# Small products of an in-kernel eigen-solver on all 128 rows of TensorE, its counting passes cut into quarters, and new places for both in the instruction order

## Chip, cores and metric

One Trainium2 chip, one core. The time is device microseconds of one launch (us), the median of the runs; one further execution was profiled.

## What is computed

The input is x of 128 graphs x 64 nodes x 128 features, and one 64 x 64 adjacency matrix for all graphs. Four residual layers follow one another, each fed by relu(layer norm(x)):

```python
x = x + L0(h, adj)   # graph convolution, two batch norms
x = x + L1(h, adj)   # two graph convolutions, then LSTMs over windows of 1, 2, 3 and 4 nodes
x = x + L2(h, adj)   # uses U of this:
    deg = sum(A, 0) + sum(A, 1) - diagonal(A)
    L_norm = dinv[:, None] * (diag(deg) - A) * dinv[None, :]
    _, U = eigh(L_norm)
    out = U @ (relu((U.T @ h) @ W1 + b1) @ W2 + b2)
x = x + L3(h, adj)   # three convolutions, 128 -> 256 -> 512 -> 128
```

The change touches only the eigendecomposition of one symmetric 64 x 64 matrix and the places of its instructions among those of L0 and L1.

## The kernel before, in words

Tokens are worked on in 4 iterations of 2048, each of 4 chunks of 512. L0 and L1 run first; L2 and L3 are one last stage ("D stage"), which needs U, as `BDU`, for its first products. All data is f32, and each matmul stands in the trace as two passes, each with its own weight load (LDWEIGHTS, engine PEld).

The eigen-solver runs beside L0 and L1, mostly on VectorE (DVE):

- 62 Householder reflections reduce the matrix `S` to a tridiagonal one. `S` has 128 rows: rows 0 to 63 are the matrix, rows 64 to 127 collect the transformation. In L0 (`reflection_beside_l0`, 28 reflections) each asks TensorE for `row_product` (L476) and `av_product` (L487); in L1 (`reflection`, 34 reflections) for one pair, `old_row` (L483) and `av_product`. Their stationary operand is a column broadcast to 128 columns, `S[0:NODES, k:k+1]`, `ident[0:NODES, ...]` or `vcol[0:NODES]`: 64 rows of the array. DVE signals `vcol` and the last column of `S` (L1289, L1290; in L0 L1208, L1212) and goes on at L1303 (L1225 in L0) when the product is there.
- `tail`: two rounds of counting. Each runs a recurrence over `Z` (128 x 65 x 32), then three passes over all of `Z`: a comparison (L1407), a comparison of neighbours (L1410) and a sum (L1414); a small product (`counts`, `sc`) follows, already with 128 rows. Then the "twist" (128 dependent tiny steps), a product of `both_ways`, the eigenvectors `V` (L1539), and six pairs or single products of 64 rows that polish U.

TensorE, DVE and ScalarE (ACT) execute in program order, so the order is the schedule. In L1, LSTM gate products are the bulk of TensorE's work: per round two sets q, each with 3 or 4 gates, of 512, 336 or 256 columns. Between gates stand "tasks" of the next or the previous chunk: `turn` and `turn_h` (transposes, 4 per chunk), `agg`, `g0`, `g1`, `agg2`. All tasks use one PSUM bank, `task_bank`; a task waits until the last one's result was taken. For `turn` and `turn_h` DVE takes it, by the addition `X<-X,PS` (L1878); for `agg2` by `T<-PS,RB` (L1817), which ACT then turns into the LSTM's input (L890).

Where the solver's instructions stand is laid out by clocks kept while the program is written. TensorE's clock (`spend`) adds the columns of each gate; when it passes `due`, the next small product is sent, `SMALL` is added, and `PACE...` gives the distance to the next. DVE's clock adds `DVE_STEP` per solver step and `busy(us)` for long ones; at each step `beside_l1` puts in at most one of L1's DVE instructions (an addition, a `BN_STATS`, a `BN_AGGR`, ...) whose time has come.

Of the kernel before, what the change touches and what calls it, by code (L numbers as in the profile page):

```python
# [21 lines left out]
ALU = mybir.AluOpType  # L22
ACT = mybir.ActivationFunctionType
AX = mybir.AxisListType.X

P = 128
GRAPHS, NODES, D = 128, 64, 128
# [14 lines left out]
M = 32  # L42
# [177 lines left out]

PACE = 3.6
PACE_AV = 6.7
PACE_GRID = [47.0, 43.0]
PACE_TWIST = 40.0
PACE_SCAN = 14.0
PACE_LAST = 8.0

SMALL = 0.5

DVE_STEP = {"reflect": 0.24, "grid": 0.16, "twist": 0.27, "tail": 0.21}  # L230

# [3 lines left out]

BEGINS = 0.5

PASS = 2.1

LN_STEP = 0.5  # L240

# [14 lines left out]
def build(nc, x_in, cst_in, w_in, adj_in, out):  # L256
    ctx = ExitStack()
    with ctx:
        def sb(name, shape):
            return ctx.enter_context(nc.sbuf_tensor(name, shape, F32))  # L260

        def sem(name):
            return ctx.enter_context(nc.semaphore(name))
# [9 lines left out]
        def C(name):  # L273
            return cst[:, coff[name][0]:coff[name][1]]
# [36 lines left out]
        S = sb("S", [P, NODES + 1])  # L311

        NI = sb("NI", [P, NODES + 2])
        vcol = sb("vcol", [P, 1])
# [9 lines left out]
        Z = sb("Z", [P, NODES + 1, M])  # L324
# [34 lines left out]
        hh_S, hh_x, hh_row, hh_v, hh_av = sem("hh_S"), sem("hh_x"), sem("hh_row"), sem("hh_v"), sem("hh_av")  # L359
# [53 lines left out]
        def eb(n):  # L413

            return PS[:, 6, n * P:(n + 1) * P]
# [35 lines left out]
        def _(pe):  # L451
            begin(pe, pe_done, pe_set)

            def mm(o, l, r, start=True, stop=True):
                return nc.tensor.matmul(o, l, r, start=start, stop=stop)  # L455

            ident = C("ident")
# [19 lines left out]
            def row_product(k):  # L477

                pe.wait_ge(hh_x, k + 1)
                mm(eb(0)[:, 0:NODES + 1 - k], S[0:NODES, k:k + 1].broadcast_to((NODES, P)),  # L480
                   NI[0:NODES, k + 1:NODES + 2]).then_inc(hh_row, 1)

            def old_row(o, k):  # L483

                n = NODES - 1 - k
                return mm(o[:, 0:n], ident[0:NODES, k:k + 1].broadcast_to((NODES, P)), S[0:NODES, k + 1:NODES])

            def av_product(k):

                pe.wait_ge(hh_v, k + 1 + max(0, k + 1 - REFLECTED))  # L490
                if REFLECTED <= k < REFLECTIONS - 1:
                    old_row(eb(3), k + 1)
                mm(eb(2)[:, 0:NODES - k], vcol[0:NODES, 0:1].broadcast_to((NODES, P)), S[0:NODES, k + 1:NODES + 1])\
                    .then_inc(hh_av, 1)

            def eigen_products(lo):


                for k in range(lo, REFLECTIONS):
                    yield PACE_AV  # L500
                    av_product(k)
# [6 lines left out]
                for n in range(ROUNDS):  # L508
                    yield PACE_GRID[n]
                    pe.wait_ge(grid_cnt, n + 1)  # L510
# [5 lines left out]

                yield PACE_TWIST
                pe.wait_ge(prep_dve, PREP["ways"])
# [63 lines left out]
            for r in range(REFLECTED):  # L582
                m = r - L0_FIRST
# [22 lines left out]

            pe.wait_ge(hh_S, REFLECTED + 1)
            old_row(eb(0)[:, (REFLECTED % 2) * NODES:], REFLECTED).then_inc(hh_row, 1)

            small = eigen_products(REFLECTED)  # L610
# [3 lines left out]
            def send():  # L614
                pace = next(small, None)
                sent.append(clock[0])
                clock[0] += SMALL
                due[0] = None if pace is None else max(due[0], clock[0] - 1.0) + pace
# [424 lines left out]
        def _(dve):  # L1043
            begin(dve, dve_done)
            v = nc.vector
# [9 lines left out]
            def busy(us):  # L1055

                dclock[0] += us

            def beside_l1(kind):

                busy(DVE_STEP[kind])
                if before_next() and l1_next[0] + lag[0] <= dclock[0]:
                    l1_next[0] = next(l1[0], None)
# [27 lines left out]
            ident, blocks = C("ident"), C("blocks")  # L1091
# [229 lines left out]
            def tail():  # L1321
# [24 lines left out]
                cn = counts[:, 0:M]  # L1346
                g = [0]

                def gop(ins):
                    g[0] += 1  # L1350
                    ins.then_inc(grid_ops, 1)

                def gsync(back=0):
                    beside_l1("grid")
                    dve.wait_ge(grid_ops, g[0] - back)

                gop(v.memset(counts[:, M:M + 1], 1.0))
                for r in range(ROUNDS):
# [45 lines left out]
                    gsync(1)  # L1404
                    gop(v.tensor_tensor(tb, Z[:, NODES, :], tb, ALU.mult))
                    gsync()
                    gop(v.tensor_scalar(Z[:, 0:NODES, :], Z[:, 0:NODES, :], 0.0, None, ALU.is_lt))  # L1407
                    gsync()
                    busy(3 * PASS)
                    gop(v.tensor_tensor(Z[:, 0:NODES - 1, :], Z[:, 0:NODES - 1, :], Z[:, 1:NODES, :], ALU.not_equal))  # L1410
                    gsync()
                    gop(v.scalar_tensor_tensor(Z[:, NODES - 1, :], xg[:, :], -1.0, tb, ALU.mult, ALU.is_gt))
                    gsync()
                    gop(v.tensor_reduce(cn, Z[:, 0:NODES, :].rearrange("p i m -> p m i"), AX, ALU.add))  # L1414
                    gsync()
                    if r == 0:

                        lanes = C("lanes").unsqueeze(1).broadcast_to(pair)
# [29 lines left out]
                ratio, inv, a, gam, hot, zt, zb, mul, t2 = (Fq[:, n, :] for n in range(9))  # L1448
# [436 lines left out]
            for k in range(REFLECTED, REFLECTIONS):  # L1885
                reflection(k)
            tail()
            assert taken[0] == len(sent)
            for _ in l1[0]:
# [109 lines left out]
```

## Time and profile before

| | |
|---|---|
| time, median of 3 runs | 953.56 us (953.52 to 959.08) |
| the profiled execution | 955.17 us, span 953.4 us |
| PE busy | 849.2 us (89%) |
| PEld busy | 558.3 us (59%) |
| DVE busy | 564.5 us (59%) |
| ACT busy | 517.3 us (54%) |
| POOL busy | 315.7 us (33%) |
| chain that ended last | PE 57%, DVE 14%, ACT 4%, POOL 2% |

The span is divided roughly so: L0 to 157 us, the passage to L1 to 178 us, L1 to 633 us, the D stage to the end. The last reflection's products are at 404 us, the counting rounds end at 461 and 506 us, the last product of the solver is at 589 us. Busy shares are averages; what a part of the change is worth is read at its place, from gaps between starts and from the waits. PEclk is TensorE's granted clock, 1.0 for 2.4 GHz and 0.5 for 1.2 GHz.

### The profile page before, as it was taken

Reading aid. Unit: us, or ns where it says so; the run is one execution under the profiler, and the core shown is the slowest. Engines: PE = TensorE matmul, PEld = TensorE weight load, DVE = VectorE, ACT = ScalarE, POOL = GpSimd, SP = SyncE. Lnnn points to the kernel's source line nnn. Section 1 sums busy time; section 2 is a strip of 40 time slices with the busy share of each in tenths; the row PEclk is TensorE's granted clock in tenths of the full one; section 3 lists DMA queues with packets and bytes.
Section 4 is the critical chain, followed back from the end, with each engine's and each line's share of the span. In section 5 each row is a group of like instructions: output and inputs, shape, how many; then the busy total and the mean of one; then the engine's idle time right before and its main releaser. Section 6 shows DMA issues by size and latency. Waiting matters only on the chain.

```text
span 953.4 us, 12338 instructions
## 1 busy us (share of the span) xinstructions
PE 849.2 (89%) x3723; PEld 558.3 (59%) x3723; DVE 564.5 (59%) x3050; ACT 517.3 (54%) x958; POOL 315.7 (33%) x373
## 2 busy tenths in 40 slices
PE   2777597798999889996899799988999999999998
PEld 1444344644687446863467545766568658858847
DVE  5899878799678977799886858436015005204101
ACT  1566585575656555664565455675364463454521
POOL 1333201375556544565564566004003002202000
PEclk9999898899999989998999899999999999999999
DMA  8000000000000000000000000000001000000101
GB/s 348 0 1 1 1 0 1 1 0 1 1 1 0 1 2 0 1 1 1 0 1 1 1 1 1 0 1 1 1 1 45 1 1 14 32 0 2 45 1 45
DMA packets 3395, 13.27 MB, mean 14 GB/s; under 512 B 512, under 2 KB 512, under 8 KB 2688
## 3 DMA queue, kind: packets, MB, share of 16 engines
q1 hardware_dynamic: 3328, 12.48, 3.3%
q8 instruction: 30, 0.49, 0.2%
q14 instruction: 37, 0.30, 0.1%
HBM read 8.28 MB, written 4.19 MB: 13 GB/s over the span
## 4 chain that ended last, share of the span: by engine, by line
PE 57%; DVE 14%; ACT 4%; POOL 2%; issue 1%; ACTq 0%; DVEq 0%
PE PS L455 56%; POOL BIG L1002 1%; ACT BIG L911 1%; DVE X L1878 1%; ACT T L877 1%; DVE Fq L1475 1%; DVE seg L1476 1%; ACT T L823 1%; PE PS L641 1%; DVE stats L1651 1%; DVE PS L1369 1%; DVE PS L1371 1%; DVE Z L1376 1%; DVE Z L1373 0%; ACT BIG L934 0%
## 5 line engine op out<-in xcount | busy, mean ns | idle before, releaser
L455 PE MATMUL PS<-BIG,wts 128*128 128x512 f32 (+2 forms) x952 | 341.3, 501 | 9.4 <-ACT BIG L911 7.0
L1002 POOL TENSOR_TENSOR BIG<-BIG 128x256 f32<-128x256 f32 (+2 forms) x220 | 211.0, 967 | 162.5 <-ACT BIG L911 96.2
L455 PEld LDWEIGHTS PS<-BIG,wts 128*128 128x128 f32 x952 | 177.4, 193 | 132.1 <-issue 95.9
L911 ACT ACTIVATE BIG<-PS,lbias 128x256 f32<-128x256 f32 (+2 forms) x312 | 162.6, 559 | 113.7 <-PE PS L455 111.6
L455 PE MATMUL PS<-H,wts 128*128 128x256 f32 (+2 forms) x312 | 115.0, 494 | 9.1 <-POOL H L1002 4.7
L815 ACT ACTIVATE BIG<-PS 128x1024 f32<-128x1024 f32 x64 | 65.5, 1023 | 88.5 <-PE PS L455 88.5
L815 ACT ACTIVATE T<-PS 128x512 f32<-128x512 f32 x96 | 55.7, 594 | 91.6 <-PE PS L455 91.3
L455 PE MATMUL PS<-T,wts 128*128 128x512 f32 x192 | 101.1, 648 | 1.7 <-ACT T L815 1.5
L1878 DVE TENSOR_TENSOR X<-X,PS 128x512 f32<-128x512 f32 x64 | 43.2, 679 | 99.3 <-PE PS L455 87.1
L979 POOL TENSOR_SCALAR rstd<-mv 128x4 f32<-128x4 f32 x48 | 11.0, 228 | 266.0 <-DVE mv L1679 266.0
L1925 DVE TENSOR_TENSOR T<-PS,wts 128x512 f32<-128x512 f32 x16 | 11.1, 691 | 142.9 <-PE PS L455 142.9
L823 ACT ACTIVATE T<-X,shift,rstd 128x128 f32<-128x128 f32 x192 | 78.4, 482 | 25.8 <-DVE shift L1688 25.8
L455 PEld LDWEIGHTS PS<-H,wts 128*128 128x128 f32 x312 | 57.6, 197 | 42.2 <-issue 19.8
L934 ACT ACTIVATE BIG<-BIG 128x512 f32<-128x512 f32 (+2 forms) x88 | 44.8, 510 | 49.1 <-POOL BIG L1002 48.3
L455 PE MATMUL PS<-wts,T 128*128 128x128 f32 (+1 forms) x384 | 60.6, 311 | 0.2
L455 PEld LDWEIGHTS PS<-wts,T 128*128 128x128 f32 x384 | 55.3, 191 | 6.8 <-issue 1.9
L455 PEld LDWEIGHTS PS<-wts,BIG 128*128 128x128 f32 x512 | 57.8, 192 | 1.9 <-issue 1.9
L455 PE MATMUL PS<-wts,BIG 128*128 128x128 f32 x512 | 57.8, 275 | 0.0
L455 PEld LDWEIGHTS PS<-T,wts 128*128 128x128 f32 x192 | 34.4, 199 | 30.6 <-issue 22.8
L981 POOL TENSOR_TENSOR rstd<-rstd,cst 128x4 f32<-128x4 f32 x48 | 49.8, 1038 | 4.0
L1672 DVE BATCH_NORM_STATS2 stats<-X 128x6 f32<-128x128 f32 x208 | 46.6, 278 | 0.7
L971 POOL TENSOR_TENSOR sc<-sc,cst 128x1 f32<-128x1 f32 x28 | 15.3, 548 | 93.8 <-DVE sc L1197 93.8
(318 smaller groups left out, 1194.9 us busy)
## 6 DMA issues: line engine op xcount, KB each, us to landing
X<-x_in SPq DMA_DIRECT2D x4, 1024.0 KB, 16.8
out<-X SPq DMA_DIRECT2D x16, 256.0 KB, 2.0
wts<-w_in SPq DMA_DIRECT2D x1, 3542.0 KB, 13.7
cst<-cst_in SPq DMA_DIRECT2D x1, 419.0 KB, 3.5
AA<-adj_in SPq DMA_DIRECT2D x2, 16.0 KB, 2.1
```

The lines of the kernel that those rows point to most:

```text
L455: return nc.tensor.matmul(o, l, r, start=start, stop=stop)
L815: nc.scalar.activation(dst, src, fn, **kw).then_inc(act_done[k], 1)
L823: j = nc.scalar.activation(T0[:, k, t * P:(t + 1) * P], X[:, a:a + P], ACT.Relu, bias=shift[:, k, t:t + 1], scale=rstd[:, k, t:t + 1])
L911: nc.scalar.activation(LB[:, q, {"i": I_, "g": G_, "f": F_, "o": O_}[g], 0:n], PS[:, 3 * q + rank[q] % 3, 0:n], ACT.Tanh if g == "g" else ...
L934: nc.scalar.activation(LB[:, q, I_, 0:n], LB[:, q, CELL, 0:n], ACT.Tanh).then_inc(act_set[q], 1)
L971: return nc.gpsimd.tensor_tensor(o, ap, mh[:, 0:1] if e is None else e, ALU.pow)
L979: nc.gpsimd.tensor_scalar(rstd[:, k, :], mv[:, k, :, 1], EPS, None, ALU.add).then_inc(pool_done[k], 1)
L981: nc.gpsimd.tensor_tensor(rstd[:, k, :], rstd[:, k, :], mh[:, 0:TPC], ALU.pow).then_inc(pool_done[k], 1)
L1002: nc.gpsimd.tensor_tensor(out, a, b, op).then_inc(pool_set[q], 1)
L1672: j = v.bn_stats(stats[:, k, t, :], X[:, a:a + P])
L1878: v.tensor_tensor(x, x, src, ALU.add).then_inc(dve_done[k], 1)
L1925: v.tensor_tensor(by_tile(T1[:, k, 0:CH]), by_tile(bank(k)), W("l2b2row").unsqueeze(1).broadcast_to(four), ALU.add).then_inc(dve_done[k], 1)
```

## The change

The three products of the reflections take all 128 rows of `S`, `NI`, `ident` and `vcol`; rows 64 to 127 of one operand are zero there (`NI` and `ident[:, k]` for k < 64, `vcol`), so the sums are the same. The three counting passes are cut into four instructions each, over quarters of the nodes (512 elements) or, for the sum, of the 32 lanes, each followed by a step in which one instruction of L1 may stand. `PASS`, `PACE_GRID`, `PACE_TWIST` and `SMALL` change the clocks by which places are laid out.

```diff
--- before.py
+++ after.py
@@ -220,12 +220,12 @@
 
 PACE = 3.6
 PACE_AV = 6.7
-PACE_GRID = [47.0, 43.0]
-PACE_TWIST = 40.0
+PACE_GRID = [52.0, 37.0]
+PACE_TWIST = 38.0
 PACE_SCAN = 14.0
 PACE_LAST = 8.0
 
-SMALL = 0.5
+SMALL = 0.45
 
 DVE_STEP = {"reflect": 0.24, "grid": 0.16, "twist": 0.27, "tail": 0.21}
 
@@ -235,7 +235,8 @@
 
 BEGINS = 0.5
 
-PASS = 2.1
+PASS = [0.25, 0.6, 0.75]
+QUARTER = NODES // 4
 
 LN_STEP = 0.5
 
@@ -477,21 +478,19 @@
             def row_product(k):
 
                 pe.wait_ge(hh_x, k + 1)
-                mm(eb(0)[:, 0:NODES + 1 - k], S[0:NODES, k:k + 1].broadcast_to((NODES, P)),
-                   NI[0:NODES, k + 1:NODES + 2]).then_inc(hh_row, 1)
+                mm(eb(0)[:, 0:NODES + 1 - k], S[:, k:k + 1].broadcast_to((P, P)), NI[:, k + 1:NODES + 2]).then_inc(hh_row, 1)
 
             def old_row(o, k):
 
                 n = NODES - 1 - k
-                return mm(o[:, 0:n], ident[0:NODES, k:k + 1].broadcast_to((NODES, P)), S[0:NODES, k + 1:NODES])
+                return mm(o[:, 0:n], ident[:, k:k + 1].broadcast_to((P, P)), S[:, k + 1:NODES])
 
             def av_product(k):
 
                 pe.wait_ge(hh_v, k + 1 + max(0, k + 1 - REFLECTED))
                 if REFLECTED <= k < REFLECTIONS - 1:
                     old_row(eb(3), k + 1)
-                mm(eb(2)[:, 0:NODES - k], vcol[0:NODES, 0:1].broadcast_to((NODES, P)), S[0:NODES, k + 1:NODES + 1])\
-                    .then_inc(hh_av, 1)
+                mm(eb(2)[:, 0:NODES - k], vcol[:, 0:1].broadcast_to((P, P)), S[:, k + 1:NODES + 1]).then_inc(hh_av, 1)
 
             def eigen_products(lo):
 
@@ -1404,15 +1403,22 @@
                     gsync(1)
                     gop(v.tensor_tensor(tb, Z[:, NODES, :], tb, ALU.mult))
                     gsync()
-                    gop(v.tensor_scalar(Z[:, 0:NODES, :], Z[:, 0:NODES, :], 0.0, None, ALU.is_lt))
-                    gsync()
-                    busy(3 * PASS)
-                    gop(v.tensor_tensor(Z[:, 0:NODES - 1, :], Z[:, 0:NODES - 1, :], Z[:, 1:NODES, :], ALU.not_equal))
-                    gsync()
+                    for a in range(0, NODES, QUARTER):
+                        busy(PASS[0])
+                        gop(v.tensor_scalar(Z[:, a:a + QUARTER, :], Z[:, a:a + QUARTER, :], 0.0, None, ALU.is_lt))
+                        gsync()
+                    for a in range(0, NODES, QUARTER):
+                        b = min(a + QUARTER, NODES - 1)
+                        busy(PASS[1])
+                        gop(v.tensor_tensor(Z[:, a:b, :], Z[:, a:b, :], Z[:, a + 1:b + 1, :], ALU.not_equal))
+                        gsync()
                     gop(v.scalar_tensor_tensor(Z[:, NODES - 1, :], xg[:, :], -1.0, tb, ALU.mult, ALU.is_gt))
                     gsync()
-                    gop(v.tensor_reduce(cn, Z[:, 0:NODES, :].rearrange("p i m -> p m i"), AX, ALU.add))
-                    gsync()
+                    for a in range(0, M, M // 4):
+                        busy(PASS[2])
+                        gop(v.tensor_reduce(cn[:, a:a + M // 4],
+                                            Z[:, 0:NODES, a:a + M // 4].rearrange("p i m -> p m i"), AX, ALU.add))
+                        gsync()
                     if r == 0:
 
                         lanes = C("lanes").unsqueeze(1).broadcast_to(pair)
```

The count of instructions on ACT, POOL and SP and their order do not change; TensorE runs the same matmuls; DVE has 18 instructions more.

DVE, round 0, from the end of the recurrence to the first `turn_h` addition (X<-X,PS), before:

```order
L1405 TENSOR_TENSOR PS<-Z,PS 128x32
L1651 BN_STATS stats<-X 128x6
L1407 TENSOR_SCALAR Z<-Z 128x2048
L1410 TENSOR_TENSOR Z<-Z 128x2016
L1651 BN_STATS stats<-X 128x6
L1412 SCALAR_TENSOR_TENSOR Z<-xg,PS 128x32
L1651 BN_STATS stats<-X 128x6
L1414 TENSOR_REDUCE counts<-Z 128x32
L1651 BN_STATS stats<-X 128x6
L1420 TENSOR_SCALAR tmp<-cst,counts 128x128
L1421 TENSOR_SCALAR sc<-sc 128x1
L1878 TENSOR_TENSOR X<-X,PS 128x512
```

The same place with the change, where the first such addition is the seventh row:

```order
L1404 TENSOR_TENSOR PS<-Z,PS 128x32
L1408 TENSOR_SCALAR Z<-Z 128x512
L1657 BN_STATS stats<-X 128x6
L1408 TENSOR_SCALAR Z<-Z 128x512
L1657 BN_STATS stats<-X 128x6
L1408 TENSOR_SCALAR Z<-Z 128x512
L1884 TENSOR_TENSOR X<-X,PS 128x512
L1408 TENSOR_SCALAR Z<-Z 128x512
L1657 BN_STATS stats<-X 128x6
L1413 TENSOR_TENSOR Z<-Z 128x512
L1657 BN_STATS stats<-X 128x6
L1413 TENSOR_TENSOR Z<-Z 128x512
```

And further on, to the second addition:

```order
L1413 TENSOR_TENSOR Z<-Z 128x480
L1657 BN_STATS stats<-X 128x6
L1415 SCALAR_TENSOR_TENSOR Z<-xg,PS 128x32
L1657 BN_STATS stats<-X 128x6
L1419 TENSOR_REDUCE counts<-Z 128x8 x2
L1663 BN_AGGR mv<-stats 128x2
L1419 TENSOR_REDUCE counts<-Z 128x8
L1884 TENSOR_TENSOR X<-X,PS 128x512
L1419 TENSOR_REDUCE counts<-Z 128x8
```

Before, the first addition stood behind all passes; now it stands inside the first pass, and the second one (right behind the first, but for statistics, before) behind three quarters of the sum.

PE, from the last LSTM iteration's rounds of 512 columns to the product of `V` (Fq), before:

```order
L455 MATMUL PS<-H,wts 128x512 x11
L455 MATMUL PS<-both_ways,cst 128x128
L455 MATMUL PS<-H,wts 128x512 x4
L641 MATMUL PS<-cst,BIG 128x128 x4
L455 MATMUL PS<-H,wts 128x512 x3
L641 MATMUL PS<-cst,BIG 128x128 x4
L455 MATMUL PS<-H,wts 128x512 x3
L455 MATMUL PS<-BIG,wts 128x512
L522 MATMUL PS<-cst,Fq 64x64
L525 MATMUL PS<-cst,S 64x64
```

and with the change:

```order
L456 MATMUL PS<-H,wts 128x512 x8
L456 MATMUL PS<-both_ways,cst 128x128
L456 MATMUL PS<-H,wts 128x512 x7
L640 MATMUL PS<-cst,BIG 128x128 x4
L456 MATMUL PS<-H,wts 128x512 x3
L640 MATMUL PS<-cst,BIG 128x128 x4
L456 MATMUL PS<-H,wts 128x512
L521 MATMUL PS<-cst,Fq 64x64
L524 MATMUL PS<-cst,S 64x64
L456 MATMUL PS<-H,wts 128x512 x2
```

The product of `both_ways` stands three gate products earlier against the gates, that of `Fq` too; the `turn_h` transposes (cst,BIG) stand where they stood against the gates.

DVE at the same part of the program, where L1539, now L1545, writes V; the first addition in the rows below is that of `turn_h` chunk 1. Before:

```order
L1537 TENSOR_SCALAR sc<-sc 128x1
L1538 TENSOR_SCALAR sc<-sc 128x1
L1878 TENSOR_TENSOR X<-X,PS 128x512
L1539 TENSOR_SCALAR Fq<-Fq,sc 128x64
L1553 COPY EV<-PS 64x64
L1554 COPY EV<-PS 64x128
L1878 TENSOR_TENSOR X<-X,PS 128x512
```

and with the change:

```order
L1543 TENSOR_SCALAR sc<-sc 128x1
L1544 TENSOR_SCALAR sc<-sc 128x1
L1545 TENSOR_SCALAR Fq<-Fq,sc 128x64
L1884 TENSOR_TENSOR X<-X,PS 128x512 x2
L1559 COPY EV<-PS 64x64
L1560 COPY EV<-PS 64x128
L1563 COPY EV<-PS 64x64
```

The addition of `turn_h` chunk 0 stood 16 solver instructions before V, outside the upper piece; it has moved behind V and stands right ahead of that of chunk 1.

Elsewhere: in round 0 the product of `counts` stands 5 gate products of 512 columns and one of 336 later, that of `sc` (round 1) one gate product of 256 columns and one task of 4 x 128 columns earlier; the first product of the tail (EV,cst) one gate product of 256 columns later. The four `T<-PS,RB` additions in the twist stand 9, 12, 12 and 8 solver instructions later, counted without the 18 new ones. In the reflections single additions move by up to four solver instructions earlier.

## Rows read from the trace of the kernel before

**Rows 1.** Windows by stage, core 0: busy us (x instructions) of each engine, PEclk, DMA share, GB/s.
```profile
108.00:157.00 49.00, 41.30 (x105) 18.02 (x104) 37.72 (x188) 34.54 (x50) 5.83 (x11) 0.90 0.00 1
178.00:404.00 226.00, 213.23 (x905) 138.45 (x903) 182.58 (x1263) 134.48 (x264) 121.84 (x124) 0.98 0.00 1
...
437.00:475.00 38.00, 27.75 (x78) 14.42 (x77) 31.18 (x130) 16.19 (x31) 19.28 (x16) 0.82 0.00 1
475.00:546.00 71.00, 63.50 (x277) 45.52 (x276) 57.08 (x248) 40.24 (x86) 38.25 (x46) 0.95 0.00 1
...
633.00:953.40 320.40, 312.39 (x1648) 223.27 (x1648) 71.23 (x306) 147.29 (x242) 35.25 (x56) 0.99 0.04 14
```

**Rows 2.** Waits, 178 to 404 us: waiter <- waited for: us in total, times, longest.
```profile
DVE sc L1303 <- PE PS L455: 37.2, 22, 4.3
...
PE PS L455 <- DVE S L1290: 7.0, 5, 2.2
```

**Rows 3.** Timeline around the small products at 304 us: start, length, instruction, [idle before].
```profile
302.32 2.31 PE L455 MATMUL PS<-H,wts 128*128 128x512 f32 x5
...
302.70 0.27 DVE L1290 TENSOR_SCALAR S<-S,sc 128x1 f32<-128x1 f32 x1
...
304.56 0.39 PE L455 MATMUL PS<-S,cst 64*128 64x15 f32 x2
...
305.10 0.30 PEld L455 LDWEIGHTS PS<-H,wts 128*128 128x128 f32 x2
...
305.64 0.19 PEld L455 LDWEIGHTS PS<-H,wts 128*128 128x128 f32 x1 [0.24 <-issue]
```

**Rows 4.** Timeline of PEld at 461 us, around two small products of 128 rows.
```profile
461.61 0.19 PEld L455 LDWEIGHTS PS<-counts,tmp 128*128 128x128 f32 x1 [0.24 <-issue]
...
461.94 0.30 PEld L455 LDWEIGHTS PS<-BIG,wts 128*128 128x128 f32 x2
462.48 0.19 PEld L455 LDWEIGHTS PS<-BIG,wts 128*128 128x128 f32 x1 [0.24 <-issue]
```

**Rows 5.** Timeline of PE, 45.5 to 48.6 us.
```profile
45.92 0.43 PE L455 MATMUL PS<-S,vcol 64*128 64x59 f32 x2 [0.62 <-DVE S L1212]
...
48.23 0.43 PE L455 MATMUL PS<-NI,S 64*128 64x59 f32 x2 [0.80 <-DVE NI L1191]
```

**Rows 6.** Timeline of PE and DVE, 127.2 to 132.5 us.
```profile
128.90 0.41 PE L455 MATMUL PS<-NI,S 64*128 64x44 f32 x2
...
131.20 0.08 DVE L1212 DVE_READ_ACCUMULATOR2_ANT S<- 128x1 f32 x1
...
132.01 0.41 PE L455 MATMUL PS<-S,vcol 64*128 64x43 f32 x2
```

**Rows 7.** Timeline of DVE, 437.5 to 450 us: the counting passes of round 0.
```profile
438.20 1.28 DVE L1407 TENSOR_SCALAR Z<-Z 128x2048 f32<-128x2048 f32 x1
439.51 3.20 DVE L1410 TENSOR_TENSOR Z<-Z 128x2016 f32<-128x2016 f32 x1
...
443.14 3.59 DVE L1414 TENSOR_REDUCE counts<-Z 128x32 f32<-128x2048 f32 x1
...
447.15 0.68 DVE L1878 TENSOR_TENSOR X<-X,PS 128x512 f32<-128x512 f32 x1
```

**Rows 8.** Timeline of PE, 436.5 to 476 us.
```profile
447.88 1.12 PE L641 MATMUL PS<-cst,H 128*128 128x128 f32 x4 [7.82 <-DVE X L1878]
448.80 6.94 PE L455 MATMUL PS<-BIG,wts 128*128 128x512 f32 x10
```

**Rows 9.** Timeline of DVE, 500 to 546 us: first and last of four additions L1817.
```profile
515.04 0.68 DVE L1817 TENSOR_TENSOR T<-PS,RB 128x512 f32<-128x512 f32 x1
...
534.68 0.68 DVE L1817 TENSOR_TENSOR T<-PS,RB 128x512 f32<-128x512 f32 x1
```

**Rows 10.** Timeline of PE and DVE, 553 to 567.5 us.
```profile
553.79 0.22 DVE L1503 TENSOR_TENSOR Fq<-PS,Fq 128x64 f32<-128x64 f32 x1 [7.78 <-PE PS L455]
...
566.59 0.24 PE L522 MATMUL PS<-cst,Fq 64*64 64x64 f32 x1 [0.28 <-DVE Fq L1539]
```

## Prediction

> **What bounds the kernel now.** I read the windows by stage first [rows 1]: from 178 to 404 us PE is busy 213.2 of 226 us at a granted clock of 0.98, while DVE stands at 81% and ACT and POOL at 60% or less. The D stage from 633 us on holds no instruction that the change touches; its 320.4 us stay. So the question is what TensorE does between 108 and 633 us, and where it stands still.
>
> Second, the waits of the reflections inside L1 [rows 2]. DVE waits 37.2 us in 22 stretches for a small product, PE waits for DVE's `S` in only 5 of 34 reflections (7.0 us). The solver is thus paced by TensorE's order in most reflections: a small product is due before TensorE reaches it, and its whole cost lies on the path.
>
> Third, that cost, from starts in the timeline [rows 3]. The passes of 512 columns follow at 0.43 us. Five begin at 302.32, so the last one ends its columns at 302.32 + 5 x 0.43 = 304.46. The next pass of 512 columns has its weight load at 305.10 and the one after it at 305.64; that one starts with the end of the pass before, so the pass's columns began at 305.64 - 0.43 = 305.21. The pair costs 305.21 - 304.46 = 0.75 us, although DVE was ready from 302.97 on, 1.6 us ahead. The first small pass starts about 0.1 us after the columns before it ended (304.56 against 304.46), with no weights loaded ahead of it.
>
> Two small products that already use 128 rows stand at 461 us [rows 4]: the last gate pass ends at 461.61, the next one begins at 462.48 - 0.43 = 462.05. Their cost is 0.44 to 0.45 us, four passes at 0.11: no gap before, none behind, weights loaded ahead.
>
> **Small products in L1 (34 pairs).** By these two rows a pair falls from 0.75 to 0.45, by 0.30. Where PE waits for DVE anyway (5 by the list; I take 6) the next reflection starts at most 0.1 earlier. 28 x 0.30 + 6 x 0.1 = 9.0. Of this I take back 1.2, four pairs' worth, for places where TensorE soon waits for POOL's or ACT's part of a round, whose chain began before the pair: 7.8. Bounds: nothing, if rows are not what makes the difference, and 34 x 0.30 = 10.2.
>
> The row shows a stop before and a late load behind a product of 64 rows between products of 128. The Trainium skill, TensorEngine Tiling (Array Packing), Key Properties, says that changing the tiling mode drains TensorE, and names 64 rows as another mode than 128. By that rule each pair pays twice; the trace agrees, 0.75 against 0.45.
>
> **Small products in L0.** In its first part (19 reflections) PE stands idle 0.62 and 0.80 us ahead of each small product, waiting for DVE [rows 5]. The array is empty then, nothing can be loaded ahead, and the chain is DVE's: 0, at most 19 x 0.1 = 1.9 from the free exit. In the second part [rows 6] `row_product` starts at 128.90, DVE signals at 131.28, and `av_product` starts only at 132.01: three gate-like halves (six passes, 2.56) lie between. Here PE is waited for, by 0.73. The product's result comes 0.2 earlier (0.1 drain, 0.1 load), and the exit of `row_product` takes 0.1 less: 0.3 per reflection. Eight of them: 2.5 (bounds 0 and 8 x 0.6 = 4.8). DVE's slack of 0.73 covers it.
>
> **Counting passes, round 0.** TensorE stopped 7.82 us before 447.88 [rows 8], because the addition that empties `task_bank` stood behind 1.28 + 3.20 + 3.59 us of passes [rows 7]. After it ten passes took 6.94 us instead of some 4.4: half clock, 2.5 lost. Together 10.5. The granted clock in 437 to 475 us is 0.82 [rows 1].
>
> With the change the first addition stands behind three quarters of the comparison. Three more recurrence steps and one more BN_STATS stand ahead: the passes begin about 0.6 late, at 438.8. Pieces of the comparison take 0.4 to 0.5, a BN_STATS between two about 0.2, so the addition starts at 438.8 + 3 x 0.4 + 2 x 0.2 = 440.4 instead of 447.15, 6.75 earlier: the stop shrinks to 1.1. But then the second addition is late. TensorE needs it one transposition and five gate products later: 441.2 + 0.4 + 5 x 0.86 = 445.9. Before it DVE has the last comparison piece with statistics (0.6 + 0.6 for the addition itself), four neighbour pieces with a BN_STATS each (3.20 / 4 plus a fixed part and 0.2, about 1.0 each: 4.0), 0.5 of small ones, and three quarters of the sum (3.59 / 4 + 0.1, 1.0 each) with a BN_AGGR: 440.4 + 1.2 + 4.0 + 0.5 + 3.1 = 449.2, done by 449.9. TensorE waits 3.8 to 4, and I charge the half clock again, 2.5. So 1.1 + 3.8 + 2.5 = 7.4 instead of 10.5: **3.1 saved**. Bounds: 10.5 if the pieces are shorter than I think and the second wait fades, -2 if both stops bring the half clock. Moving the product of `counts` into TensorE's wait at the next round start hides its 0.45: 0.4 more. The wait of DVE before its round 1 is not on the path, and the product of `sc` comes 0.43 + 0.86 = 1.3 earlier in TensorE's order; in round 1 nothing of L1 waits for the passes, and their some 1 us of added fixed cost falls into DVE's idle time ahead of `sc`.
>
> **Twist.** The four additions `T<-PS,RB` pace TensorE: ACT, in order, waits for each, and gates wait behind ACT. They run from 515.04 to 534.68 [rows 9], 82 solver steps and three additions of 0.6 apart, so 0.22 per step. They move 9, 12, 12 and 8 steps later, but the whole chain begins 1.3 earlier. The last one decides: 8 x 0.22 - 1.3 = +0.4 us. Bounds -1.3 and +1.8.
>
> **Tail.** `both_ways` is sent three gate products (2.6) earlier. DVE had waited 7.78 us for it [rows 10], so it is ready. V came 13.3 us after the product (553.3 to 566.6); without the two additions now behind it, 12.1. V is then there 2.6 + 1.2 earlier and 0.4 later, at 563.2; the addition of chunk 0 follows and ends at 563.9. TensorE wants it at about 562.3: 1.6 of waiting where 0.25 was, less the 0.3 that it waited for V before: **1.0 lost**. Bounds 0 and 3.5 (with a half clock).
>
> **Sum.** -7.8 - 2.5 - 3.1 - 0.4 + 0.4 + 1.0 = -12.4. The profiled span of 953.4 becomes 941.0. The profiled execution took 955.17, 1.6 above the median of 953.56; since two of three runs lie at 953.5, I set the change against the median: 941.2.
>
> **Rivals.**
> 1. *Rows do not matter.* The gap at 304 us could belong to the broadcast column or to the pair's place in the queue. For it: the pair at 461 us has other operands and DVE far ahead. Against it: both load 128 columns. Then only the last four terms stay, -2.1: 951.5. The Trainium skill, TensorE: Matmul & The Clock Gate, section LDWEIGHTS, gives a load's time by its columns alone and says that the count of rows doesn't matter; by this page the edit would change nothing. The passes of a pair do follow at the same 0.11 us with 64 and with 128 rows, which agrees, but the rule is silent on the entry and the exit, and there the rows differ.
> 2. *The counting stop goes entirely.* If pieces and statistics take a third less, the second addition is in time and the clock stays up: 6.3 more, 934.9. Against it: the measured 3.59 for the sum leaves little room.
> 3. *Late additions make it slower.* The mechanism: each addition delays its own round, and the delays add up instead of moving with DVE's chain. The four in the twist would cost (9 + 12 + 12 + 8) x 0.22 = 9.0, the one behind V 16 x 0.22 = 3.5, and two stops at half clock 2.5 each: 17.5, and the counting passes give nothing back. Against the 10.3 of the reflections: +7.2, 960.8, with some 4 to both sides. It decides only if TensorE stands waiting at every one of the four; against it, additions that stand closer together cannot each be late.
>
> **Chances.** My forecast 0.70, rival 1 0.14, rival 2 0.11, rival 3 0.05. The forecast's own spread, from the bounds, is 936 to 948; the range goes to 934 below and to 950 above, which leaves most of rival 1 and all of rival 3 outside. One per cent, 9.5 us, is about what can be told from no change here: under 944.0 lie rival 2 and four fifths of my own case, 0.67; over 963.1 a third of rival 3, 0.02; the rest, 0.31, lies within.
>
> **What would show it.** Around a pair, the next pass of 512 columns should begin 0.45 us after the last one ended, with its weight load 0.11 behind the small one's. In the second part of L0 `av_product` should start 2.9 after `row_product`, not 3.1 [rows 6]. The last pair should stand at 394 instead of 404 us; if it is at 404, the first two terms are wrong. Between 437 and 475 us there should be two stops of PE for X L1878, of 1 and 4 us, the second followed by half clock; one stop or none is rival 2. The four T additions should keep their spacing, and `turn_h` chunk 1 should wait 1.6 for the addition behind V.

## The result: 948.97 us, 5.0 less, where 12.4 were forecast

| | before | after |
|---|---|---|
| median of the runs (9 each) | 954.00 us | 948.97 us (944.69 to 950.66) |
| ratio after / before, 95% interval | | 0.994 (0.9921 to 0.9959) |
| the profiled execution, its span | 955.17, 953.4 | 947.86, 946.1 |
| PE busy | 849.2 us (89%) | 837.5 us (89%) |
| DVE busy | 564.5 us | 571.5 us |
| chain that ended last | PE 57%, DVE 14% | PE 55%, DVE 15% |

The time lies in the range, and the gain is less than half of the one forecast. The interval of the ratio leaves out 1, so the kernel is faster, though by less than the 1% that the prediction took as its bound. Measured again beside other kernels the ratio was 0.9931 (0.9906 to 0.9956).

**Windows by stage** of the changed kernel, columns as in [rows 1]:

```profile
178.00:404.00 226.00, 212.39 (x935) 144.28 (x935) 186.78 (x1279) 137.45 (x268) 126.80 (x130) 0.97 0.00 1
...
437.00:475.00 38.00, 32.06 (x110) 18.93 (x109) 32.26 (x157) 21.09 (x44) 17.16 (x16) 0.91 0.00 0
475.00:546.00 71.00, 60.58 (x254) 41.37 (x253) 62.33 (x249) 39.79 (x82) 40.23 (x47) 1.00 0.00 1
```

The last number but two is the granted clock. That of the counting stretch is up from 0.82 to 0.91, that of the twist from 0.95 to 1.00; in the reflections it is down, 0.97 against 0.98, though more matmuls are done.

**A pair of small products**, PE and PEld at 301 us, where [rows 3] show one of 64 rows:

```profile
299.45 1.88 PE L456 MATMUL PS<-H,wts 128*128 128x512 f32 x4
301.16 0.29 PE L456 MATMUL PS<-S,cst 128*128 128x15 f32 x2
```

The weight loads of the same moment:

```profile
300.74 0.19 PEld L456 LDWEIGHTS PS<-S,cst 128*128 128x128 f32 x1 [0.24 <-issue]
...
301.50 0.30 PEld L456 LDWEIGHTS PS<-H,wts 128*128 128x128 f32 x2
302.04 0.19 PEld L456 LDWEIGHTS PS<-H,wts 128*128 128x128 f32 x1 [0.24 <-issue]
```

Four passes of 0.43 from 299.45 end at 301.17: the small product follows with no gap, its weights loaded from 300.74 on. The gates' columns are back at 302.04 - 0.43 = 301.61. The pair costs 0.44 instead of 0.75.

**The counting passes of round 0**, DVE's timeline, for [rows 7]:

```profile
431.06 0.43 DVE L1408 TENSOR_SCALAR Z<-Z 128x512 f32<-128x512 f32 x1
431.40 0.29 DVE L1657 BATCH_NORM_STATS2 stats<-X 128x6 f32<-128x128 f32 x1
431.60 1.32 DVE L1408 TENSOR_SCALAR Z<-Z 128x512 f32<-128x512 f32 x1
432.84 0.28 DVE L1657 BATCH_NORM_STATS2 stats<-X 128x6 f32<-128x128 f32 x1
433.04 1.28 DVE L1408 TENSOR_SCALAR Z<-Z 128x512 f32<-128x512 f32 x1
434.24 0.67 DVE L1884 TENSOR_TENSOR X<-X,PS 128x512 f32<-128x512 f32 x1
434.84 1.50 DVE L1408 TENSOR_SCALAR Z<-Z 128x512 f32<-128x512 f32 x1
```

POOL's timeline of the same stretch:

```profile
431.36 2.68 POOL L1001 TENSOR_TENSOR BIG<-BIG 128x512 f32<-128x512 f32 x2 [0.74 <-ACT BIG L933]
434.78 1.28 POOL L1001 TENSOR_TENSOR BIG<-BIG 128x512 f32<-128x512 f32 x1 [0.74 <-ACT BIG L933]
```

A quarter of the comparison takes 0.43 us alone. The three that begin while POOL is at work end 0.28 us after POOL's instruction (for the last two, POOL ends at 434.04 and 436.06, the pieces at 434.32 and 436.34) and take 1.28 to 1.50. Together 4.5 us, where the whole comparison took 1.28. TensorE's stops that follow, for [rows 8]:

```profile
434.97 0.71 PE L640 MATMUL PS<-cst,H 128*128 128x128 f32 x4 [2.68 <-DVE X L1884]
443.71 0.92 PE L640 MATMUL PS<-cst,H 128*128 128x128 f32 x4 [3.74 <-DVE X L1884]
```

**The tail**, PE from 537 to 575 us, for [rows 10]:

```profile
537.93 0.38 PE L456 MATMUL PS<-both_ways,cst 128*128 128x128 f32 x2
...
544.22 2.84 PE L456 MATMUL PS<-H,wts 128*128 128x512 f32 x6 [2.48 <-POOL H L1001]
...
551.34 0.71 PE L640 MATMUL PS<-cst,BIG 128*128 128x128 f32 x4 [1.03 <-DVE X L1884]
...
552.85 0.24 PE L521 MATMUL PS<-cst,Fq 64*64 64x64 f32 x1
...
573.41 2.28 PE L456 MATMUL PS<-H,wts 128*128 128x336 f32 x4 [2.22 <-POOL H L1001]
```

`turn_h` waits 1.0 for the addition behind V, but two round starts wait 2.5 and 2.2 us for POOL as well (1.45 and 1.60 before), and behind the second the clock falls: windows give 0.84 for 575 to 582 us.

Starts of the same instructions in the two traces give the account by stretch; a product that stands earlier in TensorE's order is set back by the gate columns it was moved past (1.3 us at `sc`, 2.56 at `both_ways`):

| stretch | forecast | profile | second profile |
|---|---|---|---|
| L0, to the last `row_product` (156.8, 154.4) | -2.5 | -2.3 | -3.9 |
| reflections in L1 (to 407.1, 398.9) | -7.8 | -5.8 | -7.8 |
| counting, with the product of `counts` (to 506.3, 494.4) | -3.5 | -2.4 | -2.4 |
| twist (to 553.3, 537.9) | +0.4 | -2.2 | -2.2 |
| tail, to the first `BDU` product (633.8, 625.0) | +1.0 | +3.9 | +3.9 |
| D stage | 0 | +1.5 | +1.5 |
| sum | -12.4 | -7.3 | -10.9 |

The second profile is of the same kernel (run after_again, 944.28 us); its runs lay at 944.0 to 944.3 (four) and at 948.3 to 952.7 (five). The two profiles part in L0 (granted clock 0.70 in one, 0.80 in the other, from 108 to 125 us) and above all between 215 and 250 us, at one pair of small products; see the late pairs below. The profiled execution of before was 1.2 over its median and that of after 1.1 under its own, which is why 7.3 becomes 5.0.

### The profile page after: what moved, and what is told of

It reads as the page before. It is cut to its first block, busy times and chain, and to the rows that moved or that the text cites. A ratio compares the mean times of both kernels' runs of the same rounds, so it can differ in the third digit from the quotient of the medians.

```text
span 946.1 us, 12357 instructions
## 1 busy us (share of the span) xinstructions
PE 837.5 (89%) x3723; PEld 559.4 (59%) x3723; DVE 571.5 (60%) x3068; ACT 516.1 (55%) x958; POOL 312.6 (33%) x373
## 4 chain that ended last, share of the span: by engine, by line
PE 55%; DVE 15%; ACT 5%; POOL 2%; issue 1%; ACTq 0%; DVEq 0%
PE PS L456 54%; POOL BIG L1001 2%; ACT BIG L910 1%; ACT T L876 1%; DVE X L1884 1%; DVE Fq L1481 1%; DVE seg L1482 1%; ACT T L822 1%; DVE stats L1657 1%; PE PS L640 1%; DVE PS L1368 1%; DVE PS L1370 1%; DVE Z L1375 1%; DVE Z L1372 0%; ACT T L814 0%
## 5 line engine op out<-in xcount | busy, mean ns | idle before, releaser
L1001 POOL TENSOR_TENSOR BIG<-BIG 128x256 f32<-128x256 f32 (+2 forms) x220 | 207.9, 953 | 159.8 <-ACT BIG L910 94.2
L456 PE MATMUL PS<-T,wts 128*128 128x512 f32 x192 | 104.3, 667 | 1.5 <-ACT T L814 1.0
```

The source lines that it names most:

```text
L1001: nc.gpsimd.tensor_tensor(out, a, b, op).then_inc(pool_set[q], 1)
```

## Experiments

All times below are medians, compared by their ratio to the kernel before on the same chip (955 us there). First each part of the change alone, then with one part undone.

**Rows alone.**

```diff
+                mm(eb(0)[:, 0:NODES + 1 - k], S[:, k:k + 1].broadcast_to((P, P)), NI[:, k + 1:NODES + 2]).then_inc(hh_row, 1)
...
+                mm(eb(2)[:, 0:NODES - k], vcol[:, 0:1].broadcast_to((P, P)), S[:, k + 1:NODES + 1]).then_inc(hh_av, 1)
```

> The kernel before with nothing changed but the products of the reflections, on 128 rows. Theory A (the forecast's terms hold and what is missing was lost among the places after the reflections): the last pair at 404 us comes some 8.4 us earlier, as in the changed kernel, and nearly all of it is kept: 944 to 947 us. Theory B (every gain in front of a wait is partly given back at the next stop of TensorE, at half clock too): the last pair is 8 us earlier, but the time falls by 5 or less, 949 or more. Theory C (rows do nothing, the gain is the passes'): 953 to 954.

Measured 945.2 us, ratio 0.9902 (0.9879 to 0.9925): -9.4, faster than the changed kernel. The forecast for its two terms was -10.3; by the median, theory A. Its profile is of the slowest of its six runs (951.46 us) and shows a gain of 3.7 only: the last pair is 7.4 us earlier, and 3.8 of that go between 421 and 436 us, with TensorE at half clock (granted 0.80 in 415 to 432 us). Four transpositions take 0.96 to 1.12 us there instead of 0.60 to 0.66:

```profile
424.57 1.12 PE L634 MATMUL PS<-cst,T 128*128 128x128 f32 x4 [0.62 <-DVE X L1876]
...
428.89 0.96 PE L634 MATMUL PS<-cst,T 128*128 128x128 f32 x4
```

So theory B's mechanism exists too, in some executions. The order of TensorE's and DVE's instructions is the same here as before, so the two traces can be set side by side pair by pair: at 24 of the 34 pairs in L1 the gate products around the pair stand 0.28 to 0.31 us closer. The other ten lie beside a wait or a change of the clock.

**Rows undone** (the same lines the other way, in the changed kernel).

> The changed kernel with its reflection products on 64 rows again; passes in pieces and new places stay. Theory A (passes save about 2, places lose about as much or more): 954 to 957 us. Theory B (gains shrink, places cost little): 951 to 953. If passes and places give the 3 that were forecast for them less 1 for the tail: 951.5.

Measured 955.1, ratio 1.0001 (0.9987 to 1.0015), theory A by the time: pieces and places together give nothing.

**Pieces alone** (`PASS` and the three loops of the diff in the kernel before).

> The kernel before with its counting passes in four pieces each and the clock's costs for them, the four numbers of the places as before. Both theories: one stop of TensorE of 7.8 us at 440 becomes two of 2.9 and 3.9, the granted clock in 437 to 475 us rises from 0.82 to about 0.91, gain 2.3 at that place. Theory A: 951 to 952 us. Theory B: what is gained is lost at the round start behind it, 953 to 954.

Measured 953.25, ratio 0.998 (0.9969 to 0.9992): -1.9, between the two theories. Its trace has stops of 2.67 and 2.69 us.

**Places alone.**

```diff
-PACE_GRID = [47.0, 43.0]
-PACE_TWIST = 40.0
+PACE_GRID = [52.0, 37.0]
+PACE_TWIST = 38.0
...
-SMALL = 0.5
+SMALL = 0.45
```

> The kernel before with only the four numbers of the places changed (52, 37, 38 and 0.45), 64 rows and whole passes. Theory A (the places cost what is missing): 956 to 959 us, with longer stops of TensorE at the start of the round that follows the product of both_ways and for chunk 1 of turn_h. Theory B (the places are nearly free): 953 to 955.

Measured 953.3, ratio 0.9978 (0.9962 to 0.9994): -2.1; theory B by its time. Of A's two stops the first is there (2.4 us for POOL behind `both_ways`, 1.45 before, with half clock behind it), the one for chunk 1 of `turn_h` is not. The places gain at another spot and lose behind `both_ways`. PE in this run, where the kernel before waits 7.82 [rows 8]:

```profile
444.74 0.74 PE L641 MATMUL PS<-cst,H 128*128 128x128 f32 x4 [4.17 <-DVE X L1878]
```

With whole passes the addition now stands between the second and the third. Pieces and places cure the same stop, so their gains don't add. The starts of the same gate products in the traces, against the kernel before, show it for the stretch from 420 to 506 us (the -2.4 of the account above is for a longer one, from 407 us on):

| | change of the stretch, us |
|---|---|
| pieces alone, old places | -3.3 |
| places alone, whole passes | -4.3 |
| rows and places, whole passes (below) | -4.3 |
| pieces and places, with or without the rows | -1.7 |

**The changed kernel again**, as the measure for the next three.

> The changed kernel once more, beside the next three on one chip. If the 5.0 us gained were the draw of a few runs, its ratio leaves 0.992 to 0.996; if not, it is there again. It is the measure for the three kernels beside it.

Measured 948.3, ratio 0.9931: the gain is there again.

**Whole passes in the changed kernel** (the passes' lines of before, rows and places kept).

> The changed kernel with its counting passes whole again; 128 rows and the new places stay. Theory A (the new places alone already put the first addition between the second and the third pass, as in the run of the places alone: one stop of 4.3 us and 1.7 at half clock instead of 2.9 + 3.9 and 1.3; the pieces then cost more than they give): 1 to 2.5 us faster than the changed kernel. Rival (the pieces are worth the 3.1 of the forecast): 3 slower than the changed kernel.

Measured 944.4, ratio 0.9889 (0.9875 to 0.9903): by the median 4 us faster than with the pieces. Its DVE:

```profile
427.38 1.23 DVE L1405 TENSOR_SCALAR Z<-Z 128x2048 f32<-128x2048 f32 x1
...
428.73 3.12 DVE L1408 TENSOR_TENSOR Z<-Z 128x2016 f32<-128x2016 f32 x1
...
432.06 0.68 DVE L1876 TENSOR_TENSOR X<-X,PS 128x512 f32<-128x512 f32 x1
```

The product of `sc` comes 2.7 us earlier than in the second profile of the changed kernel. Behind `both_ways` a stop of 2.7 us for chunk 1 of `turn_h` (1.03 there) and what follows take all of it back: both spans are 942.5 us. The four runs lie at 944.0 to 944.5, as the lower four of the changed kernel do, so the traces give the whole passes nothing in the end. The 4 us of the median stand because five of nine runs of the changed kernel lie at 948.3 to 952.7, and none of four here.

**Only the comparison whole.**

```diff
+                    gop(v.tensor_scalar(Z[:, 0:NODES, :], Z[:, 0:NODES, :], 0.0, None, ALU.is_lt))
+                    for a in range(4):
+                        busy(PASS[0])
+                        beside_l1("grid")
```

> The changed kernel with the comparison as one instruction again, the L1 instructions that stood between its pieces behind it in the same sequence; the other two passes stay in pieces. Theory A (a piece of the comparison that starts while POOL works takes until POOL is done, 1.3 to 1.5 us instead of 0.43; the four took 4.5 us in round 0, the whole 1.28): the first addition comes some 1.9 us earlier, the second some 3, the two stops of TensorE of 2.9 and 3.9 fall to 1.0 and some 2.5: 2.5 to 3.5 us faster than the changed kernel. Rival (the time of those passes is covered by other waits): within 1 us of the changed kernel.

Measured 950.7, ratio 0.9952 (0.9934 to 0.9969): neither theory, 2 us slower. The first stop fell to 1.0 us as expected, the second grew to 4.1, where 2.5 were expected. DVE's timeline:

```profile
432.19 0.67 DVE L1414 TENSOR_TENSOR Z<-Z 128x512 f32<-128x512 f32 x1
...
432.98 1.55 DVE L1414 TENSOR_TENSOR Z<-Z 128x512 f32<-128x512 f32 x1
...
435.45 1.51 DVE L1414 TENSOR_TENSOR Z<-Z 128x480 f32<-128x480 f32 x1
```

Now pieces of the neighbours' comparison wait for POOL: the collisions moved on. Even so the stretch to 506 us is 0.3 us shorter than in the changed kernel; the loss comes behind `both_ways`, where `turn_h` waits 2.68 us for the addition instead of 1.03. Three instructions of V's chain on DVE take 1.11, 1.29 and 1.33 us there, where the changed kernel has 0.25, 0.29 and 1.20.

**The comparison's pieces in another form.**

```diff
-                        gop(v.tensor_scalar(Z[:, a:a + QUARTER, :], Z[:, a:a + QUARTER, :], 0.0, None, ALU.is_lt))
+                        gop(v.tensor_scalar(Z[:, a:a + QUARTER, :], Z[:, a:a + QUARTER, :], 0.0, None, ALU.is_lt, ALU.add,
+                                            accum_out=cn[:, 0:1]))
```

> The changed kernel with its comparison pieces in the form that also writes out a sum of what it compared (into a column that is overwritten later); all else the same. Theory A (the plain form of the piece can't run while POOL works, the form with a sum can): each of the eight pieces takes 0.55 to 0.7 us, whatever POOL does, where three took 1.28 to 1.50 in round 0 and two 1.00 in round 1. Rival (a piece is slow for its own size, or POOL slows any instruction of DVE): pieces beside POOL's work take 1.2 us or more again. Time: within 2 us of the changed kernel, 946 to 949.

Measured 948.1, ratio 0.992 (0.9892 to 0.9949), as expected. DVE's timeline:

```profile
428.70 0.67 DVE L1408 TENSOR_SCALAR_CACHE_REDUCE Z<-Z 128x512 f32<-128x512 f32 x1
...
429.50 0.67 DVE L1408 TENSOR_SCALAR_CACHE_REDUCE Z<-Z 128x512 f32<-128x512 f32 x1
...
431.51 1.75 DVE L1414 TENSOR_TENSOR Z<-Z 128x512 f32<-128x512 f32 x1
```

POOL's:

```profile
428.19 2.50 POOL L1001 TENSOR_TENSOR BIG<-BIG 128x512 f32<-128x512 f32 x2 [0.74 <-ACT BIG L933]
431.44 1.27 POOL L1001 TENSOR_TENSOR BIG<-BIG 128x512 f32<-128x512 f32 x1 [0.74 <-ACT BIG L933]
```

All eight pieces take 0.67 to 0.69 us, seven of them with POOL at work beside them: theory A, the plain form and POOL exclude each other. The first piece of the neighbours' comparison, which reads two operands in SBUF, still waits (1.75). The Trainium skill, SBUF — State Buffer, Who interferes with whom, has this rule: VectorE and GpSimd share one port pair as an exclusive lock; `tensor_scalar` may take it, its form with an accumulator and reductions don't, two SBUF inputs contend with a GpSimd instruction that reads SBUF. The traces agree on each: 1.28 to 1.50, 0.67, 1.5 to 1.75, and 0.99 to 1.08 for each piece of the sum.

**Rows and pieces, old places** (the four numbers as before).

> The kernel before with rows and pieces, the four numbers of the places as before: with the rows alone (ratio 0.990), the passes alone (0.998) and the changed kernel (0.993 to 0.994) beside it. Theory A (the places behind both_ways are what costs): 0.986 to 0.989 of before, 941 to 944 us. Rival (rows and pieces are in each other's way): 0.992 or more.

Measured 948.2, ratio 0.9921 (0.9902 to 0.994): the rival's time. Against rows alone (0.9902) the pieces cost 1.8 by the medians, but the intervals overlap: not settled. From 436 to 506 us the pieces give 0.4 in its trace beside that of rows alone, with stops of 2.68 and 4.31 us, where pieces alone give 3.3 with stops of 2.67 and 2.69.

**The product of `both_ways` back at its place**: `PACE_TWIST = 41.4` for 38.0.

> The changed kernel with PACE_TWIST 41.4 instead of 38: the product of both_ways and what follows stand where they stood before. Theory A (the places behind both_ways cost 4: stops of 2.6, 1.2 and 2.4 us at 541, 550 and 571 us instead of 1.6, 0.3 and 1.8, and a stretch of half clock at 574): 3 to 4 us faster than the changed kernel, the stops as before. Rival (the tail's product only moves the waiting from V to the addition, as forecast, 1.0): 0 to 1 faster.

Measured 941.45, ratio 0.9863 (0.9848 to 0.9879): 6.5 faster than the changed kernel by the medians, more than theory A gave. PE:

```profile
541.21 2.84 PE L456 MATMUL PS<-H,wts 128*128 128x512 f32 x6 [2.49 <-POOL H L1001]
...
566.86 0.33 PE L456 MATMUL PS<-EV,cst 64*64 64x64 f32 x2 [0.57 <-DVE EV L1578]
568.82 3.38 PE L456 MATMUL PS<-H,wts 128*128 128x336 f32 x11 [0.87 <-POOL H L1001]
```

The wait at 541 stays, so that one is not this place's. The waits of 1.0 for the addition and of 2.2 for POOL are gone or halved, and the clock is 1.00 in 575 to 582 us. From `both_ways` to the first `BDU` product it loses 0.7 us where the changed kernel loses 3.9. That is 3.2 us, as theory A had it. The spans differ by 6.3, but 3.0 of these are there before `both_ways`, where the two programs are the same instruction by instruction: they are a difference between executions, and the edit is worth some 3.2 of the 6.5.

**Only the products behind it back**: `PACE_SCAN = 17.4` for 14.0.

> The changed kernel with PACE_SCAN 17.4 instead of 14: the product of both_ways stays early, the product of Fq and all that follow stand where they stood before. Theory A (it is the addition for chunk 1 of turn_h that stands behind DVE's whole chain of V, because that chain is sent early): the stop of 1.2 us at 550 and what follows it stay, 947 to 949 us. Rival (it is the polish products in the gates' order behind it): as fast as with PACE_TWIST 41.4, 941 to 943.

Measured 946.5, ratio 0.9901 (0.9881 to 0.992): between the two theories. By starts the stop at 550 is 1.2 us as in the changed kernel, that at 571 is 1.8 instead of 2.4, and the clock stays at 1.00 behind it. From `both_ways` to the first `BDU` product this trace loses 1.6 us, between 3.9 and 0.7: by it 2.3 of the cost are the products behind, 0.9 the place of `both_ways` itself.

**Whole passes and the old place together** (both edits above).

> The changed kernel with whole counting passes and with PACE_TWIST 41.4, both of the edits that were faster when made alone (944.4 and 941.5 against 948.3). If the whole passes keep the 2.7 us that they are ahead at the product of sc: 938.5 to 939.5. If they are lost again at the next wait, as they were behind both_ways in the run of the whole passes: 941 to 942.

Measured 941.0, ratio 0.9841 (0.982 to 0.9861). Against 0.9863 that is 2 us, with intervals that overlap: not settled.

**The late pairs later.** The two profiles of the changed kernel differ most at one stop. DVE, POOL and PE before the pair at 229 us in the first profile, each in its own timeline:

```profile
223.68 1.28 DVE L1638 SCALAR_TENSOR_TENSOR lnv<-lnv 128x16 f32<-128x16 f32 x1
```
```profile
223.67 3.83 POOL L1001 TENSOR_TENSOR BIG<-BIG 128x512 f32<-128x512 f32 x3 [1.47 <-ACT BIG L910]
```
```profile
229.00 0.62 PE L456 MATMUL PS<-S,cst 128*128 128x26 f32 x2 [3.00 <-DVE S L1289]
```

and the same three in the second profile:

```profile
223.01 0.17 DVE L1638 SCALAR_TENSOR_TENSOR lnv<-lnv 128x16 f32<-128x16 f32 x1
```
```profile
223.00 3.89 POOL L1001 TENSOR_TENSOR BIG<-BIG 128x512 f32<-128x512 f32 x3 [1.47 <-ACT BIG L910]
```
```profile
227.06 0.40 PE L456 MATMUL PS<-S,cst 128*128 128x26 f32 x2 [1.72 <-DVE S L1289]
```

In both profiles DVE's instruction starts 0.01 us behind one of POOL's; once it takes 1.28 us, once 0.17. TensorE then stands 3.0 us instead of 1.7, and the granted clock of 225 to 235 us is 0.70, where the second profile has 1.00. DVE waits for TensorE again at the next pairs, so nothing asks for that stop but the pair's place. The edit is made in the changed kernel with `PACE_TWIST` 41.4; it was not tried in the kernel before:

```diff
+PACE_AV, LATER = 6.7, {33: 0.85, 35: -0.85, 36: 2.0, 37: -2.0, 50: 1.7, 52: 1.0, 53: -1.0, 54: -1.7}
...
-                    yield PACE_AV
+                    yield PACE_AV + LATER.get(k, 0.0)
```

> The changed kernel with PACE_TWIST 41.4 and those pairs of small products in L1 for which TensorE waits for DVE (at 206, 213, 229, 319 and 333 us) one to three gate products later in its order, the next ones as much nearer. Theory A (these waits of 0.8, 0.8, 1.9 to 3.2, 2.3 and 1.6 us and the half clock behind them are lost for nothing, since DVE is ahead by 1 to 3 us again one or two pairs on): 5 to 8 us faster than with PACE_TWIST alone, 934 to 937. Rival (the solver's chain through DVE sets the time there and the waits come back at the next pairs): 940 to 942.

Measured 931.3 us (930.95 to 935.65), ratio 0.9758 (0.9738 to 0.9777), with `PACE_TWIST` 41.4: 23 faster than before by the ratio, 10 faster than with that number alone. Waits, 178 to 404 us, and the window, against [rows 2] and [rows 1]:

```profile
DVE sc L1302 <- PE PS L456: 20.9, 19, 2.2
...
PE PS L456 <- DVE S L1289: 2.6, 4, 1.9
```
```profile
178.00:404.00 226.00, 216.70 (x968) 148.11 (x967) 195.49 (x1335) 141.86 (x279) 133.04 (x139) 0.99 0.00 1
```

PE waits 2.6 us for `S` instead of 7.0 (8.0 in the changed kernel), and is busy 3.5 us more of the same stretch. Of the five stops of the changed kernel (0.7, 0.6, 3.0, 2.1 and 1.4 us) two are left, 0.3 and 1.9; the 5.4 us of waits taken away do not come back at the next pairs. This profile is of the slowest of the four runs (935.65 us): against that of `PACE_TWIST` 41.4 alone it is 5.6 us ahead at 400 us and 5.9 at the end, so the rest of the 10 us is in executions that were not profiled.

**Only the pair at 229 later**, in the changed kernel: `LATER = {36: 2.0, 37: -2.0}`.

> The changed kernel with one pair alone, the one at 229 us, two gate products later and the next as much nearer. Theory A (that stop, 3.2 us in one profile and 1.9 in another of the same kernel, and the fall of the clock behind it split the runs into some at 944 and some at 949 to 952): all runs at 941 to 944, median 5 to 6 us below the changed kernel's 948.3. Rival (the spread comes from other places, such as the stops of 2.3 and 2.1 us at 318 and 343 us): the median falls by the stop alone, 1.2 to 2, and the spread stays 8 us.

Measured 943.4 (942.08 to 944.47), ratio 0.9876 (0.9862 to 0.989): theory A. The stop is 0.57 us. One pair, moved by two gate products, is worth 5 us in the median, and none of its four runs is in the upper group; against the lower group of the changed kernel (944.0 to 944.3) it is worth 0 to 2. That the whole passes too had four runs at 944.0 to 944.5 without this edit, and that the run with `PACE_TWIST` 41.4 has the stop of 3.0 us in a profile of 941.6, keep me from calling the grouping settled.

**All of it.**

> Whole counting passes, PACE_TWIST 41.4 and the late pairs later, on the changed kernel: every edit that was faster alone. In the runs so far whole passes gave 2 us beside PACE_TWIST 41.4 (ratio 0.984 against 0.986) and the late pairs 10 us (0.976 against 0.986). If they add up: 929 to 930 us. If the whole passes are worth nothing once the rest stands right: 931 to 932.

Measured 933.0, ratio 0.9768 (0.9755 to 0.978): no better than with the pieces (0.9758), and the intervals overlap. The version to keep is that of the late pairs with the passes in pieces.

## Why the prediction was off

The time that the small products give was forecast well. What is missing was lost behind them: in the tail (the step "1.0 lost", 3.9 in the traces), in the D stage ("its 320.4 us stay", 1.5 longer), at one pair in L1, and between pieces and places, which together save less than either alone. Two sums in the working are also a little high: 7.82 + 2.5 is 10.3 and not 10.5, eight times 0.3 is 2.4 and not 2.5; with them the forecast is -12.1.

- **Small products in L1 and L0: right.** 0.45 for 0.75 at each pair, forecast for sum -10.3; rows alone gave -9.4. "Where PE waits for DVE anyway ... the next reflection starts at most 0.1 earlier" left out that the pair at 229 could wait longer than before (3.0 us; no wait of PE for `S` was longer than 2.2 [rows 2]), and that the clock falls there: -5.8 instead of -7.8 in one profile, -7.8 in the other. What in a product of 64 rows costs the 0.30 us, the stop before it or the late load behind it, no run separates. The L0 rows came as forecast, `av_product` 2.90 behind `row_product` (128.43, 131.33).
- **Counting passes: wrong, the step "Pieces of the comparison take 0.4 to 0.5".** Three of four took 1.3 to 1.5, because POOL was at work. The first addition came at 434.24, with the passes beginning at 431.06: 3.2 behind their start instead of 1.6. The first stop was 2.7, not 1.1; the second 3.7 as forecast. Half clock cost 1.5 (six passes in 4.27 us instead of 2.74) instead of 2.5. So 7.9 us of loss came close to the 7.4 forecast, but by luck: 1.6 more at the first stop, 1.0 less by the clock. The larger miss is that the new numbers move the addition in front of the third pass by themselves; I had read the places for the products alone. Either part alone shortens the stretch by 3.3 or 4.3 us, both by 1.7, so at the new places the pieces cost 2.7 us up to the product of `sc`, and the next stop behind `both_ways` hides that. By medians the pieces are worth -1.9 alone, where -3.1 was forecast; the +1.8 beside the rows and the +4 beside rows and places are within what the executions of one kernel differ by.
- **Twist: sign wrong, little in it.** The four additions kept their spacing, 505.49 to 524.87, which is 19.4 for 19.6 [rows 9]; the stop behind them was 2.5 us instead of 3.4 by starts, and the half clock behind it (granted 0.57 in 539 to 547 us before, 1.00 in 530 to 538 now) did not come again: -2.2 for +0.4. The term had no clock in it.
- **Tail: wrong, the step "1.0 lost".** The wait for the addition behind V is there, 1.03 us; the two that follow it, at a round start for POOL (1.8 to 2.4 by starts) and the half clock behind it, were not in the term. DVE had V 12.8 us behind the product of `both_ways` (550.69), near the 12.1 of the forecast; TensorE took it only at 14.9 (552.85), because its product stands behind the `turn_h` that waits. The trace gives +3.9 for the stretch, +0.7 with the old place: the new place costs 3.2, where 1.0 was forecast.
- **D stage: "its 320.4 us stay" was wrong by 1.5.** Its first 32 passes took 5.44 us instead of 3.81, at half clock (granted 0.72), with no instruction changed. The same stands in 12 of the 16 profiles other than that of before, with old places and with new ones. Rows alone and pieces alone keep their gain from there to the end (3.7 and 3.7; 2.8 and 2.9 in their profiles). What decides it stays open.
- Rival 1 is refuted by rows alone; rival 2 did not happen; rival 3's mechanism (stops grow where TensorE stands waiting) happened in the tail alone.

## What to carry to other kernels

Where two engines follow a fixed order, look for waits after which the waited-for engine is soon idle again: such a wait is bought back by moving the request one to three steps later, and here five such moves were worth about as much as the cheaper request (10 us and 9.4 by medians). Before a DVE pass is cut into pieces, see what POOL does meanwhile, since each piece may wait for an instruction of POOL's once. A sum of gains holds only as long as each is at a stop of its own: measure the parts alone and with one left out. Where executions of one kernel differ by 8 us, set two traces side by side before a median of four runs is put down to an edit: what differs ahead of the edit is not its work.

## What the runs showed that was not expected

- DVE and POOL exclude each other for some forms: a DVE instruction of 0.17 us takes 1.28, one of 0.43 takes up to 1.50 and ends 0.28 us behind POOL's; the form with a sum took 0.67 to 0.69 in all eight pieces. The wait stands in the trace as the instruction's own length, not as idle time before it.
- Such a collision hangs on hundredths of a us: in both profiles DVE's L1638 begins 0.01 us after POOL's instruction, once it waits and once it doesn't, and around the longer stop the granted clock is 0.70 over 10 us instead of 1.00.
- A pair of products of 64 rows between products of 128 costs 0.28 to 0.31 us more than on 128 rows, at 24 of the 34 pairs in L1.
